# An attention and expert layer on one core: prologue with queries first, four help tiles on VectorE, extra pieces placed anew, last columns stored alone

## The reference

```python
q, k, v = heads(xn @ Wq.T), heads(xn @ Wk.T), heads(xn @ Wv.T)   # 16 heads of 8
q = q * cos + rotate_half(q) * sin
k = k * cos + rotate_half(k) * sin
attn = softmax(einsum('bhnd,bhmd->bhnm', q, k) * 8 ** -0.5)
attention = einsum('bhnm,bhmd->bhnd', attn, v)
gates = softmax(xn @ gate_w + gate_b); top 2 of 8 experts per token
expert = gelu(gelu(xn @ w1 + b1) @ w2 + b2) @ w3 + b3            # 128, 256, 256, 128
experts = sum over the two experts of gate * expert
```

## Time and profile before

| | us |
|---|---|
| median of three runs | 628.67 |
| the profiled execution | 628.49 |
| its span | 626.7 |
| first exponential | 24.37 |
| steps 0 and 1 | 24.37 to 86.75 |
| steps 2 to 8 | 86.75 to 296.4 |
| experts | 296.4 to 424.44 |
| steps 9 to 15 | 424.44 to 619.1 |

### The profile page before, as it was taken

How to read it: one execution, slowest core, us unless ns; L and a number is a source line. 1 busy time by engine, 2 the same in 40 slices (tenths; PEclk the granted TensorE clock), 3 DMA queues, 4 the chain that set the end, 5 groups by cost and what they waited for, 6 DMA issues and landing times.

```text
span 626.7 us, 12150 instructions
## 1 busy us (share of the span) xinstructions
PE 595.1 (95%) x4128; PEld 255.9 (41%) x4128; DVE 335.7 (54%) x795; ACT 536.0 (86%) x548; POOL 196.6 (31%) x187
## 2 busy tenths in 40 slices
PE   8889999999999999999999999998999999999996
PEld 6323332232222222232899999983222222222221
DVE  5654322776263335021565555546394958668475
ACT  3799999999999999999455555559999999999995
POOL 2700000000444544441122222223655748484000
PEclk9999999999999999999999999999999999999998
DMA  7653711443264626693433333310312112131311
GB/s 231 171 197 133 264 44 35 162 159 119 85 223 164 219 85 227 205 296 76 99 75 81 71 73 75 75 44 19 110 35 84 59 59 67 55 87 55 116 40 38
DMA packets 82622, 70.69 MB, mean 113 GB/s; under 512 B 44288, under 2 KB 58400, under 8 KB 82576
## 3 DMA queue, kind: packets, MB, share of 16 engines
q1 hardware_dynamic: 76000, 56.34, 29.7%
q0 software_dynamic: 5856, 13.05, 6.8%
q10 hardware_dynamic: 720, 0.71, 0.5%
HBM read 32.92 MB, written 32.96 MB: 105 GB/s over the span
## 4 chain that ended last, share of the span: by engine, by line
PE 62%; ACT 17%; issue 12%; DVE 5%; DMA 2%; ACTq 0%; SPq 0%; DVEq 0%
PE ps L1491 11%; PE ps L1425 10%; ACT probs L729 9%; PE ps L1475 7%; PE ps L1548 6%; ACT probs L694 5%; PE ps L1417 5%; PE ps L1438 5%; PE ps L1521 4%; PE ps L1398 4%; ACT probs L672 2%; PE ps L1343 2%; PE ps L1378 2%; PE ps L1306 1%; DVE x_all L1176 1%
## 5 line engine op out<-in xcount | busy, mean ns | idle before, releaser
L694 ACT ACTIVATE probs<-ps 128x1536 f32<-128x1536 f32 (+1 forms) x154 | 205.2, 1435 | 3.3 <-PE ps L1475 2.9
L729 ACT ACTIVATE probs<-ps 128x1536 f32<-128x1536 f32 x140 | 190.2, 1516 | 2.1 <-PE ps L1521 1.9
L572 POOL DMA_INDIRECT slots_x_d<-xn_all,slot_i x64 | 63.4, 991 | 191.7 <-DVE expert_i L1033 125.0
L1491 PE MATMUL ps<-probs,v_st 128*32 128x512 f32 x896 | 119.3, 605 | 0.6 <-ACT probs L694 0.6
L708 ACT ACTIVATE work<-ps,work 128x256 f32<-128x256 f32 (+1 forms) x156 | 64.9, 455 | 60.4 <-PE ps L1425 60.2
L1548 PE MATMUL ps<-probs,v_st 128*32 128x512 f32 x840 | 111.4, 604 | 0.5 <-DVE o_sb L918 0.5
L610 POOL DMA_INDIRECT work<-slots_y_d,slot_i x64 | 89.8, 1404 | 64.7 <-PE ps L1548 48.5
L1475 PE MATMUL ps<-q_st,k_st 32*128 32x512 f32 x448 | 77.2, 494 | 6.2 <-ACT probs L694 4.5
L1521 PE MATMUL ps<-q_st,k_st 32*128 32x512 f32 x420 | 71.1, 494 | 8.8 <-ACT probs L729 8.7
L1475 PEld LDWEIGHTS ps<-q_st,k_st 32*128 32x128 f32 x448 | 28.9, 181 | 118.9 <-ACT probs L694 91.0
L1521 PEld LDWEIGHTS ps<-q_st,k_st 32*128 32x128 f32 x420 | 26.4, 181 | 108.0 <-ACT probs L729 99.0
(11 more groups left out here) (193 smaller groups left out, 552.8 us busy)
## 6 DMA issues: line engine op xcount, KB each, us to landing
k_d<-parts SPq DMA_DIRECT2D x8, 1024.0 KB, 4.6
q_d<-parts SPq DMA_DIRECT2D x8, 1024.0 KB, 5.2
q_st<-q_d SPq DMA_DIRECT2D x30, 256.0 KB, 3.4
k_st<-k_d SPq DMA_DIRECT2D x30, 256.0 KB, 3.0
slots_x_d<-parts SPq DMA_DIRECT2D x5, 1024.0 KB, 7.5
work<-slots_x_d SPq DMA_DIRECT2D x128, 32.0 KB, 1.9
slots_y_d<-work POOLq DMA_DIRECT2D x32, 128.0 KB, 2.2
work<-work SPq DMA_DIRECT2D x24, 128.0 KB, 2.0
```

Of the source, the lines that this page charges most:

```text
L694: nc.scalar.activation(group_probs(phase, g)[:, 0:size, :], group_slot(g)[:, 0:size * HALF].rearrange("p (h n) -> p h n", n=HALF), ACT.Exp ...
L729: nc.scalar.activation(late_probs(g), group_slot(g).rearrange("p (h n) -> p h n", n=HALF), ACT.Exp, scale=SCALE).then_inc(S["exp_done"], 1)
L1491: ins = nc.tensor.matmul(o_ps[32 * h:32 * h + 32, :], v_window(mt, h, half), group_probs(phase, half * HALF_GROUPS + g)[:, n, :], start=(j ...
```

## The change

1. **Prologue.** The layernorm's chain is shorter (two instructions fewer ahead of the square root, two fewer behind it). TensorE warms with 7 matmuls instead of 10, and then 2, and the small matmuls between the transposes and the four (`WARM_AGAIN`) ahead of the first scores are gone. Queries are projected first, then the first 256 keys, then the other 256, the second half's keys, values, and the second half's queries. The first queries are rotated and split by ScalarE and VectorE; 256 keys (`START_KEYS`) go through as a piece of their own and are loaded alone. The table load for the exponential is behind the first copy of the transposed rows. VectorE makes the high parts of the second half's keys and copies half of the first values.
2. **Extra pieces.** "plain", "norm", "count", the joins and the route steps have new blocks; from step 3 on the "turn" stands at place 6 instead of 4 (place 14 in step 2). ScalarE's exponential for the routing is in group 14 of step 2 instead of group 11. The load of the second half's keys no longer waits for the stored queries.
3. **Late steps 9 to 14.** The help tiles are those of the first half of the queries, and all four are VectorE's: four reads, then the eight instructions on 128x2048, the power in place in `probs`. ScalarE's L733 stays in step 15 alone. `combine` is behind `normalise`, for both gathers at once, and the gathered rows have two buffers.
4. **End.** The last half's output is copied and transposed in two pieces, and the final addition and the store are of the last 32 columns alone; the other 96 columns are stored before.

```diff
-    fixed = {0: ("values", 0, 2), 7: ("norm", 0), 64: ("norm", 1), 94: ("norm", 2), 126: ("norm", 3), 54: ("count",),
+    fixed = {0: ("values", 0, 2), 7: ("norm", 0), 60: ("norm", 1), 92: ("norm", 2), 120: ("norm", 3), 52: ("count",),
...
-ROUTE_EXP = (2, 11)
+ROUTE_EXP = (2, 14)
...
+            first_load(1, S["q0_loaded"])
...
+            sp.dma_start(k_st[:, 0:START_KEYS].bitcast(F32), parts[0:P // G, 0, :, 0:START_KEYS].bitcast(F32)).then_inc(S["k00_loaded"], 16)
+            first_load(0, S["ka_loaded"], START_KEYS, HALF)
...
-                    if g == HELP_AT + 5:
+                    if last and g == HELP_AT + 5:
                         act.wait_ge(S["help_scored"], (t - SPLIT) * HG + HG)
                         nc.scalar.activation(help_probs[:, 0, :], aux_ps, ACT.Exp, scale=SCALE).then_inc(S["help_exp"], 1)
...
-            def read_help(t):
-
-                for k in range(3):
+            def read_help(t, tiles):
+
+                for k in range(tiles):
                     dve.wait_ge(S["help_scored"], (t - SPLIT) * HG + k + 1)
                     nc.vector.tensor_scalar(he_s[:, k * HALF:(k + 1) * HALF], aux_ps, SCALE / math.log(2), EXP_SHIFT, ALU.mult, ALU.add)\
                         .then_inc(S["help_read"], 1)
-                    if t > SPLIT and k < 2:
-                        combine(t - SPLIT - 1, k)
...
-                read_help(t)
+                read_help(t, HG)
...
-                help_exps(t)
+                help_exps(t, HG)
                 if t > SPLIT:
                     normalise(t - 1)
+                    combine(t - SPLIT - 1)
...
+            finish_early_columns().then_inc(S["out_ready"], 1)
+            tail_copy()
+            tail_finish()
...
-            for _ in range(WARM_AGAIN):
-                nc.tensor.matmul(bank(0), zeros[:, 0:P], xnT[:, 0, 0:HALF], start=True, stop=True)
+            pe.wait_ge(S["proj_read"], 3)
+            scores(0, 0, first=True)
+            project_values(0, 1, v0_ps[1]).then_inc(S["v0_done"], 1)
             pe.wait_ge(S["proj_read"], 4)
-            scores(0, 0, first=True)
...
                     if j < BLOCKS - 1:
+                        scores(t, j + 1)
                         if (t, j) == (0, 0):
                             pe.wait_ge(S["v0_read"], 2)
-                            pe.wait_ge(S["wT_copied"], 3)
-                        scores(t, j + 1)
+                            pe.wait_ge(S["wT_copied"], 4)
```

More of the change, by code:

```diff
@@ L717, in _, with late_exps @@
             nc.scalar.activation(fb[:, 3:4], zeros[:, 0:1], ACT.Exp)
-            def late_exps(t, first=False):
+            def late_exps(t, first=False, last=False):
                 for g in range(LATE_GROUPS):
@@ L735, in _ @@
             late_exps(SPLIT, True)
-            with act.Fori(SPLIT + 1, STEPS) as t:
+            with act.Fori(SPLIT + 1, STEPS - 1) as t:
                 late_exps(t)
+            late_exps(STEPS - 1, last=True)
             act.wait_ge(S["flag_made"], 1)
@@ new lines, in turn_start_keys @@
+            def turn_start_keys(piece, table):
+                cols = slice(piece * START_KEYS, (piece + 1) * START_KEYS)
+                done, signal = (("k00_proj", "k00_read"), ("proj_done", "proj_read"))[piece]
+                dve.wait_ge(S[done], (1, 3)[piece] + table)
+                dst, src = (t_cos, t_sin)[table], (cos_sb, sin_sb)[table]
+                ins = nc.vector.tensor_tensor(dst[:, 0, cols], proj_ps[0][:, table * HALF + cols.start:table * HALF + cols.stop], src[:, cols], ALU.mult)
+                if table:
+                    ins.then_inc(S[signal], 1)
@@ new lines, in _, with turn_first_rows @@
+            ins.then_inc(S["wT_made"], 1)
+            for _ in range(WARM_ROWS):
+                nc.tensor.matmul(aux_ps[:, 0:HALF // 2], zeros[:, 0:P], zeros[:], start=True, stop=True)
+            def turn_first_rows(half):
+                for k in range(4 * half, 4 * half + 4):
+                    pe.wait_ge(S["rows_made"], k + 1)
+                    ins = nc.tensor.transpose(bank(half)[:, (k % 4) * C:(k % 4 + 1) * C], xn_all[:, k, :], ident)
+                ins.then_inc(S["trans_done"], 1)
@@ L1301, in first_projection, with project_start_keys @@
                                      start=True, stop=True).then_inc(S["proj_done"], 1)
+            def project_start_keys(piece):
+                lo, hi = piece * START_KEYS, (piece + 1) * START_KEYS
+                if piece:
+                    pe.wait_ge(S["k00_read"], 1)
+                for s in range(2):
+                    nc.tensor.matmul(proj_ps[0][:, s * HALF + lo:s * HALF + hi], weights(0, s), xnT[:, 0, lo:hi],
+                                     start=True, stop=True).then_inc(S[("k00_proj", "proj_done")[piece]], 1)
@@ L1364, in scores @@
                     pe.wait_ge(S["k00_loaded"], 16)
-                if (j == 0 and not (first and t == 0)) or (isinstance(t, int) and (t, j) == (0, 1)):
+                if (j == 0 and not (first and t == 0)) or (isinstance(t, int) and (t, j) == (0, 2)):
                     pe.wait_ge(S["ka_loaded"], t * 16 + 16)
@@ L1400, in values, with turn @@
                 ins.then_inc(S["pv_done"], 1)
-            def turn(t, half=0, helped=False):
-                if helped:
-                    pe.wait_ge(S["help_exp"], t - (SPLIT - 2))
+            def turn(t, half=0, helped=None):
+                if helped == "late":
+                    pe.wait_ge(S["help_read"], (t - (SPLIT - 2)) * HG)
+                elif helped == "last":
+                    pe.wait_ge(S["help_exp"], 1)
                 free_aux(aux_of_turn(t, half))
@@ L1517, in late_scores @@
                     pe.wait_ge(S["kb_loaded"], t * 16 + 16)
+                if not last and (1, 0, 0) in items:
+                    pe.wait_ge(S["q1_loaded"], t * 16 + 16)
                 if g >= 2 or not first:
@@ L1562, in late_step @@
                     if g < LATE_GROUPS - 1:
-                        late_scores(t, g + 1, first=(first and g == 0))
+                        late_scores(t, g + 1, first=(first and g == 0), last=last)
                     elif not last:
@@ L1571, in late_step @@
                     if HELP_AT <= g < HELP_AT + HG:
-                        help_scores(t, g - HELP_AT)
-                    if g == HELP_AT + 7 and not first:
-                        turn(t - 1, 0, True)
+                        help_scores(t, g - HELP_AT, last)
+                    if g == 9 and not first:
+                        turn(t - 1, 0, "last" if last else "late")
                     if g == 13 and last:
```

349 lines of the change are left out of this document (208 added, 141 removed).

## The result

The changed kernel takes 632.16 us in the median of five runs (631.48 to 632.43), beside 628.63 (628.26 to 629.24) for the kernel before on the same chip. The ratio is 1.0055, with a 95% interval of 1.0043 to 1.0067. It is slower by 3.5 us. The forecast was 628.2, with a range that ended at 631.2: the prediction was wrong.

What follows compares the result with a forecast made beforehand. ScalarE was taken to set the pace, TensorE close behind. Prologue -3.2, steps 2 to 8 +0.6, late steps +3.1 and end -0.9 sum to -0.4: 628.2 us, own range 627.0 to 629.5, 8-in-10 range 625.2 to 631.2.

Steps and rivals of the forecast that it cites:

- Step 3: Count piece moved to group 5: TensorE waits 1.6 us for VectorE's masks, a third early piece costs 0.4; +2.0.
- rival D: Prologue: TensorE's clock falls to 1.2 GHz with less warming, some 3 us more, 631.2 us; chance 0.08.
- Rival C: Masks are ready when TensorE asks, as VectorE runs ahead through step 2; 1.6 goes, 626.6 us; chance 0.17.
- Late steps: Steps 9 to 14: VectorE's chain grows to 16.4 us, TensorE waits some 1.4, steps of 28.3; +3.2 or +3.1.
- Rival A: Late steps: VectorE keeps up, 2048-element operations cost about what 1536 do; steps 26.9, 620.0 us; chance 0.06.
- Rival B: Late steps: VectorE's chain is 16.9 us instead of 16.4, +3.0, 631.2 us; chance 0.13.
- Prologue: Before step 1: first exponential 3.9 us earlier, third scores at 24.4 instead of 27.63 behind `v0_read`; -3.2 (-1.5 to -3.9).
- The rest of steps 2 to 8: Steps 2 to 8 without step 3: -0.4 in step 2, -1.1 in step 4, +0.1 in steps 5 to 8.
- Step 2: ScalarE no longer waits for the routing's input, its exponential now being in group 14; -0.4 (0 to -0.8).
- step 4: Scores wait less for keys as joins end earlier, and the norm piece is gone; from 31.00 us, -1.1.
- End: After the last step: transposes 0.2 earlier, final addition 0.3 instead of 0.69, store -0.3; -0.9 in all.
- the smaller store: End: a quarter store, 64 KB in as many pieces, takes 0.3 us less; an estimate between 0 and -1.

Runs made afterwards that it cites:

- two fillers: Changed kernel plus two matmuls on zeros ahead of the count piece's wait for the masks in step 3: 629.33 us (1.0018 to the kernel before).
- five: Changed kernel plus five matmuls on zeros ahead of the count piece's wait for the masks in step 3: 629.83 us (1.0020 to the kernel before).
- the kernel before with the wait put in: Kernel before, with only the count piece at block 52 of step 3, turn at place 6 and route steps earlier: 633.67 us (1.0091).

## Why the prediction was wrong, point by point

- **Step 3, +2.0 forecast, +5.1 measured: the step that failed.** The prediction summed "the masks come at 10.1, and TensorE waits 1.6" and 0.4 more. Wait, cause and place were right (10.2 and 1.79), and so was the price of a wait (1.8 with two fillers, 2.2 with five). The missing 3.0 is TensorE's work at 1.2 GHz behind it, a term that the sum put at nothing. With the profiles' numbers step 3 adds up: 29.62 before, 0.2 for the pieces' new places (0.4 forecast), 1.8 for the wait, 3.1 for the clock, 34.7. The kernel before had no idle time of TensorE over 0.91 from step 1 on, and its clock row showed no fall but at its very end; the prediction priced a fall in the prologue alone, as rival D, and never asked for it where it had itself put the longest idle time. The rule that it cited there (Trainium skill, "TensorE: Matmul & The Clock Gate", What's actually happening: the clock is given back when the engine idles) holds at this place: idle 1.79, then 0.51. By itself it does not say where the clock falls: the waits of 1.19 to 1.31 in the late steps brought no fall. Rival C is out, since TensorE did wait. Rival D had the right mechanism at the wrong place.
- **Late steps, +3.1 forecast, +2.4 measured.** The mechanism held: 2.29 and 1.23 an operation, the chain 16.44, and 3.06 from the help values to the next step's start. The first read starts 3.55 instead of 3.73 into the step and the fourth at 7.90 instead of 8.02, so the chain ends at 25.06 (25.2 forecast), TensorE waits 1.2 (1.4 forecast), and the steps are 28.18 instead of 28.3. Rival A is out: an operation on 2048 elements takes 2.29, one on 1536 takes 1.76. Rival B's longer chain is out too: it is 16.44, not 16.9. The kernel did get slower, but not by B's way.
- **Prologue, -3.2 forecast, -2.2 measured.** The first exponential came 2.8 earlier, but the third scores 2.2 (25.45 instead of 27.63, where 24.4 was forecast), held by the wait for `v0_read` as said. Two sizes were off. The rows started at 8.67, not 8.2, and the first scores at 20.96, not 19.9. TensorE computes the first values behind these scores, and VectorE copies them ahead of the logits: it waited 1.20 for them, began the copy at 22.40, and made `v0_read` at 23.74 instead of 22.7. The keys' sum on GpSimd, which the forecast took for the last input, ended at 22.03 (21.7 forecast). In three of the nine profiles with this prologue a fall of the clock there put off step 1 by some 1.5 more; in the changed kernel's own it did not.
- **The rest of steps 2 to 8, -1.4 forecast, -1.0 measured.** Step 2 got 0.7 shorter (0.4 forecast) and step 4 0.9 (1.1 forecast). Step 6 got 0.8 longer and steps 5, 7 and 8 together 0.2 shorter, where +0.1 was forecast for the four.
- **End, -0.9 forecast, -0.6 measured.** Copy 0.2 and addition 0.4 came as summed. The 0.3 for the smaller store did not come: 3.5 us in both kernels. By the page named in the prediction (Trainium skill, "DMA: Bandwidth & Descriptors", Specifications: below 512 bytes a piece is read before it is written) the gain would be nothing, and between the two kernels it was. But against a whole store in the same kernel the quarter was 0.6 faster, so this does not show that the size of the pieces is the reason.

With these 3.0 in the sum the forecast would have been 631.2, and slower. The other misses add up to 1.0 more: prologue and rest gained 1.4 less than forecast and the end 0.3 less, while the late steps cost 0.7 less, which hid part of it.

## What to carry to other kernels

When a change makes TensorE wait in the middle of dense work, price the wait and, separately, the work behind it at half clock: here 1.8 and 3.0. The busy row does not show it, the count of matmuls and the granted clock do. A helper engine's chain pays until its end meets the moment at which it is asked for; three tiles with 4.4 us to spare beat four that came 1.2 late, by 4.7 us over six steps. And split a change into its parts: moving the additions alone gained 2.5 us, which the fourth tile hid.

## What was not expected of the hardware

The clock's fall does not follow from the length of one idle time alone. Behind 1.79 and 2.81 us in step 3 it came in both profiles that had such a wait. Behind 1.19 to 1.32 in the late steps it never came, in any of the eight profiles with these waits, nor behind 1.29 between the first two blocks' scores of the kernel before:

```profile
25.54 0.50 PE L1378 MATMUL ps<-q_st,k_st 32*128 32x512 f32 x4 [1.29 <-ACT probs L672]
```

In the changed prologue it came in one profile behind 0.47 and in two behind 0.78, while other executions with the same idle times there kept the full clock. And it stays down for different times: 6.9 us in the changed kernel's step 3, 3.5 in the kernel before with the wait put in and in the three falls in the prologue. What decides between these stays open.
